# Order of a tile's two transposes in a mixture-of-experts stage: h transposed behind the next tile's first product

## What is computed

```python
def _L0_ffn_ref(x, gate_w, gate_b, bias, w1, b1, w2, b2):
    E, TOP_K, D, H = (8, 2, 512, 352)
    xf = x.reshape(-1, d)
    scores = xf @ gate_w.T + gate_b + bias
    top_scores, top_idx = jax.lax.top_k(scores, TOP_K)
    gates = jax.nn.softmax(top_scores, axis=-1)
    ...
    h = jax.nn.silu(jnp.einsum('td,ehd->teh', xf, w1) + b1)
    y = jnp.einsum('teh,edh->ted', h, w2) + b2
    out = jnp.einsum('ted,te->td', y, comb)
```

## Time and profile before

| | us |
|---|---|
| median of 3 runs (1011.74 to 1012.09) | 1011.93 |
| the profiled execution, whole | 1011.67 |
| its span in the trace | 1010.0 |
| PE busy | 996.3 |
| DVE busy | 686.4 |
| ACT busy | 514.0 |
| POOL busy | 259.3 |
| expert stage, first product of h(0) to the end | 815.7 to 1010.0 |

### The profile page before, as it was taken

The page is one execution under the profiler, slowest core; times in us unless marked ns, Lnnn a source line. Parts: engine busy times, 40 slices in busy tenths (PEclk is TensorE's granted clock), DMA queues, the critical chain, the costliest instruction groups (busy, mean ns, idle before and its releaser), DMA issues.

```text
span 1010.0 us, 17489 instructions
## 1 busy us (share of the span) xinstructions
PE 996.3 (99%) x5029; PEld 840.0 (83%) x5030; DVE 686.4 (68%) x1552; ACT 514.0 (51%) x1324; POOL 259.3 (26%) x413
## 2 busy tenths in 40 slices
PE   8999999999999999999999999999999989999998
PEld 7888888888888888888788888888888879988996
DVE  7888655565666667667877878777887665544544
ACT  4545444454444457755555555555554954343442
POOL 1000000000000002222423233333333645656564
PEclk9999999999999999999999999999999999999999
DMA  7002501000000011343221111111125635555653
GB/s 262 23 21 84 209 27 36 21 21 21 21 22 21 21 63 63 104 173 116 43 53 49 45 42 42 42 42 42 42 73 161 187 119 101 108 102 99 110 107 48
DMA packets 46861, 75.35 MB, mean 75 GB/s; under 512 B 6089, under 2 KB 18554, under 8 KB 46690
## 3 DMA queue, kind: packets, MB, share of 16 engines
q1 hardware_dynamic: 37010, 56.04, 18.0%
q0 software_dynamic: 9808, 18.79, 10.1%
HBM read 53.14 MB, written 23.50 MB: 76 GB/s over the span
## 4 chain that ended last, share of the span: by engine, by line
PE 93%; DVE 3%; ACT 2%; DMA 1%; issue 1%; SPq 0%; POOL 0%; POOLq 0%; DVEq 0%; ACTq 0%
PE pK L1614 16%; PE pK L1616 16%; PE pK L1615 16%; PE pA L1614 6%; PE pA L1616 6%; PE pA L1615 6%; PE pX L1614 6%; PE pX L1616 5%; PE pX L1615 5%; PE pA L1748 3%; PE pT L1958 2%; PE pT L1694 2%; PE pX L1976 1%; PE pA L1882 1%; DVE w_lo L1523 1%; PE pT L1629 1%
## 5 line engine op out<-in xcount | busy, mean ns | idle before, releaser
L965 ACT ACTIVATE qs<-q,nrec 128x64 f32<-128x64 f32 x512 | 129.6, 336 | 88.0 <-DVE nrec L1344 87.9
L586 POOL TENSOR_TENSOR wv_lo<-wv_in,wv_hi 128x512 fp32r<-128x512 f32 x4 | 5.2, 1292 | 403.0 <-ACT wo_hi L886 403.0
L1614 PE MATMUL pA<-k_hi,xn_hi 128*128 128x512 f32 x256 | 101.0, 394 | 0.5 <-DVE k_lo L1219 0.5
L1614 PE MATMUL pK<-wq_hi,xnT_hi 128*128 128x512 f32 x256 | 100.4, 392 | 0.0
L1614 PE MATMUL pK<-wk_hi,xnT_hi 128*128 128x512 f32 (+1 forms) x256 | 100.1, 391 | 0.2 <-DVE xnT_lo L1199 0.2
L1616 PE MATMUL pK<-wq_hi,xnT_lo 128*128 128x512 f32 x256 | 99.9, 390 | 0.0
L1616 PE MATMUL pA<-k_hi,xn_lo 128*128 128x512 f32 x256 | 99.8, 390 | 0.0
L1615 PE MATMUL pK<-wk_lo,xnT_hi 128*128 128x512 f32 (+1 forms) x256 | 99.7, 390 | 0.0
L1615 PE MATMUL pA<-k_lo,xn_hi 128*128 128x512 f32 x256 | 99.7, 389 | 0.0
L1616 PE MATMUL pK<-wk_hi,xnT_lo 128*128 128x512 f32 (+1 forms) x256 | 99.7, 389 | 0.0
L1615 PE MATMUL pK<-wq_lo,xnT_hi 128*128 128x512 f32 x256 | 99.7, 389 | 0.0
(11 more groups left out here) (277 smaller groups left out, 2447.7 us busy)
## 6 DMA issues: line engine op xcount, KB each, us to landing
w_in<-in_ffn_w SPq DMA_DIRECT2D x22, 256.0 KB, 3.6
w_in<-in_ffn_w SPq DMA_DIRECT2D x8, 704.0 KB, 7.6
xn<-in_attn_hidden_states SPq DMA_DIRECT2D x16, 256.0 KB, 6.3
wv_in<-in_attn_Wv SPq DMA_DIRECT2D x16, 256.0 KB, 2.8
wo_in<-in_attn_Wo SPq DMA_DIRECT2D x16, 256.0 KB, 3.0
wk_in<-in_attn_Wq SPq DMA_DIRECT2D x4, 1024.0 KB, 5.7
xnT_dram<-xnT SPq DMA_DIRECT2D x4, 1024.0 KB, 11.6
x_in<-in_attn_hidden_states SPq DMA_DIRECT2D x16, 256.0 KB, 2.6
```

Of the source, the lines that this page charges most:

```text
L965: i = nc.scalar.activation(qs[:, s], q[:, s], ACT.Copy, scale=nrec[:, b * HC + h:b * HC + h + 1])
L1614: nc.tensor.matmul(dst, lhs[0], rhs[0], start=start, stop=False)
```

## The change

In PE's order, hT(i-1) now stands behind h(i) and ahead of gT(i+1); it was hT(i) behind y(i-2). ACT's and DVE's orders follow: ACT takes the copy of h(i), the cast of gT(i+1), then silu of tile i-1. DVE takes gT_lo(i+1), hT_hi and hT_lo of tile i-1, then the scaling of y(i-2). PE's order is now: h(0), gT(1), h(1), hT(0), gT(2); then h(i), hT(i-1), gT(i+1), y(i-2); then h(38), hT(37), y(36), hT(38), y(37), y(38). The matmuls, copies and transfers are the same ones.

```diff
-            def act_tile_e(i, e=None, last=False):
-                act_h(i)
-                if not last:
-                    act_gT(i + 1)
-                if e is None:
-                    e = act.value_load(tile_expert[0:1, ds(i, 1)], min_val=0, max_val=E - 1)
-                act_silu(i, e)
+            def act_tile_e(i):
+                act_silu(i, act.value_load(tile_expert[0:1, ds(i, 1)], min_val=0, max_val=E - 1))
...
-            act_tile_e(0, first_expert)
-            with act.Fori(1, NS - 1) as i:
-                act_tile_e(i)
-            act_tile_e(NS - 1, last=True)
+            act_h(0)
+            act_gT(1)
+            act_h(1)
+            act_gT(2)
+            act_silu(0, first_expert)
+            with act.Fori(2, NS - 1) as i:
+                act_h(i)
+                act_gT(i + 1)
+                act_tile_e(i - 1)
+            act_h(NS - 1)
+            act_tile_e(NS - 2)
+            act_tile_e(NS - 1)
...
             with dve.Fori(2, NS // 2) as h:
                 for b in range(2):
                     dve_gT(2 * h + (b + 1))
+                    dve_hT(2 * h + (b - 1), 1 - b)
                     dve_y(2 * h + (b - 2), b, 16 * h - 16)
-                    dve_hT(2 * h + b, b)
+            dve_hT(NS - 2, 1)
             dve_y(NS - 3, 0, 16 * (NS // 2) - 16)
             dve_hT(NS - 1, 0)
             dve_y(NS - 2, 1, 16 * (NS // 2) - 16)
...
             pe_h(0, first_experts[0])
             pe_gT(1, 1)
+            pe_h(1, first_experts[1])
             pe_hT(0)
-            pe_h(1, first_experts[1])
             pe_gT(2, 0)
-            pe_hT(1)
             pe.wait_ge(w_lo_ready, len(DVE_STEPS))
             with pe.Fori(1, NS // 2) as h:
                 for b in range(2):
                     i = 2 * h + b
                     pe_h(i, expert(i))
+                    pe_hT(2 * h + (b - 1))
                     pe_gT(2 * h + (b + 1), 1 - b)
                     pe_y(2 * h + (b - 2), b, expert(2 * h + (b - 2)))
-                    pe_hT(i)
             pe_h(NS - 1, expert(NS - 1))
+            pe_hT(NS - 2)
             pe_y(NS - 3, 0, expert(NS - 3))
```

More of the change, by code:

```diff
@@ L1587, in _ @@
             dve_gT(1)
-            dve_hT(0, 0)
             put_gates()
             dve_gT(2)
-            dve_hT(1, 1)
+            dve_hT(0, 0)
             dve.wait_ge(gates_ready, 1)
@@ L1595, in _ @@
                 dve_gT(i + 1)
+                dve_hT(i - 1, 1 - i % 2)
                 dve_y(i - 2, i % 2, 0)
-                dve_hT(i, i % 2)
             with dve.Fori(2, NS // 2) as h:
```

## The result

The changed kernel takes **1013.77 us** (median of 22 runs, 1013.23 to 1015.15), the kernel before in the same comparison 1012.03 (22 runs, 1011.6 to 1012.81). The ratio is 1.0017, with a 95% interval of 1.0012 to 1.0023: +1.7 us where +0.7 was forecast. The profiled execution took 1013.59 us and spans 1011.9.

What follows compares the result with a forecast made beforehand. PE, dense with work between the pipeline's filling and its end, was taken to bound the kernel. Loop -0.3, start +0.34 and end +0.6 gave +0.65, rounded to +0.7 us: 1012.6 us from 1011.93, 8-in-10 range 1011.3 to 1014.0.

Steps and rivals of the forecast that it cites:

- the sum: Whole kernel: loop, start and end terms together +0.65, rounded to +0.7 us, from 0.0 to +1.5; chance 0.88.
- The start: PE's gap before gT(2): hT(0) leaves the first gap and delays the copy of h(1) and all up to h(2), +0.34 us.
- The seams: Transitions between PE's groups in each steady tile: all four cost at most 0.02 us of 4.78; -0.3 us taken over 36 tiles.
- Rival (b): PE's exit from transposes to products costs array time: one exit less gives 0.09 us a tile, 1009.7 us; chance 0.04.
- The loop: Steady tiles, h(3) to h(38): only the seams between PE's groups change the time, -0.3 us, between -0.7 and +0.2.
- The end: Behind h(38): hT(37) on the path +0.33, new wait before y(37) +0.45, wait before y(38) -0.2; +0.6 us, +0.3 to +1.0.
- The covers: Slack in the loop before PE would wait: 0.44 us for gT_lo ahead of h, 1.8 for hT_lo ahead of y; no cost.
- Rival (a): Every steady tile: gT_lo late for h(i+1), ACT's copy queued behind hT(i-1); 0.1 us beyond cover gives 1016.2 us; chance 0.07.
- Rival (c): Steady loop: seven grouped transposes lower PE's clock to 1.2 GHz, up to twice the 167 us, near 1180 us; chance 0.01.

## Why the prediction was right, and where it was not

**The outcome.** No difference above 0.2%, on the slower side, inside the range of 8 in 10: right, with the interval's upper end at 0.23%. The size was off, +1.7 us for +0.7, and that is above the sum's own bounds, +1.5 us or 1013.4. The range held because it was drawn wider than the sum, for mis-sized seams and handovers. Of what came, two parts had no term in the sum, a change of h's rhythm and a slow read on PE's sequencer, and that they stayed within the added width is luck.

**The start: right.** +0.35 us against +0.34. h(2)'s first product came at 824.32, forecast near 824.3. The two kernels in which hT(0) went back into the gap show it alone: 8.22 and 8.23 us from h(0) to h(2), before 8.21.

**The seams: right, at less.** The seams gave back 5 ns a tile, 0.17 us in all, where the forecast -0.3 is 8 ns a tile. Rival (b), a dear way out of transposes, fell with the period that it would have shortened: a tile is 4.79 us, not 4.69.

**The loop: the step that failed.** The term for the steady loop, -0.3 us between -0.7 and +0.2, was a sum of seams alone; measured is +0.54. It took h's spacing of 0.158 us from the one tile of the earlier trace rows and held it for given, whatever stands ahead of h. It isn't: ten steps took 1.58 to 1.61 us in the kernel before, by expert, and with a product or a single transpose ahead of h some tiles at odd places take 1.66. That made +0.71 us of the stretch in one execution and about +1.0 in the other. Shown are the two conditions: the kernel before with only the seam changed has slow tiles, three transposes ahead take them away, even places take them away, odd places for all experts spread them to experts of both kinds. What in the chip makes the rhythm, and why it takes one tile and spares the next, no run settles.

**The end: a mis-sized term.** With T the start of hT(37), 998.89, the reckoning holds nearly to its last step. PE was there at T + 2.76 (forecast 2.75), silu at T + 1.30 (1.2), hT_lo's end at T + 3.15 (3.05). But y(37) started at T + 3.62, not T + 3.2. The wait was 0.86 us and not 0.45: 0.1 from the silu, the rest the read of the expert number behind the wait for silu(37), which the prediction costed on ACT and left out on PE. The kernel with early reads puts it at 0.32. With a read of 0.3 us the omission would have cost nothing, as the two kernels with one transpose ahead show; the read took 0.68. hT(37) took its 0.33, and y(37) to y(38) went from 2.37 to 2.19, -0.18 for a forecast -0.2. Together 0.33 + 0.86 - 0.18 = +1.0, the upper bound of the term. The last scatter followed y_last's scaling by 0.78 us as before (1007.07 + 0.75 to 1008.60), so the reading of y_last in the prediction holds.

**The covers: right.** gT_lo ended at 852.60 and h followed at 853.17, with 0.57 between, 0.14 of it the handover: 0.43 of cover, forecast 0.44. The longer ACT chain gave 0.35 to 0.45. hT_lo's, from the changed kernel's DVE to the y(i-1) that reads it at 855.76, is 1.83 of a forecast 1.8:

```profile
851.91 0.69 DVE L1202 TENSOR_TENSOR gT_lo<-pT,gT_hi 128x512 fp32r<-128x512 f32 x1 [2.00 <-ACT gT_hi L1127]
...
853.37 0.56 DVE L1202 TENSOR_TENSOR hT_lo<-hT,hT_hi 128x384 fp32r<-128x384 f32 x1
```

Rival (a) was 0.43 us away.

**The clock: right.** The changed kernel from 829 to 1000 us (us, busy time of each engine, granted clock, DMA share, GB/s), seven transposes in a row in each tile:

```profile
829.00:1000.00 171.00, 171.00 (x1001) 156.27 (x1000) 82.35 (x143) 64.83 (x176) 89.76 (x69) 1.00 0.56 99
```

It is 1.00, and so is that of the kernel with ten transposes a tile. Rival (c) fell. The Trainium skill ("TensorE: Matmul & The Clock Gate", section "Part 4: PE-mode transpose") says that the full clock does not engage for transposes; in this kernel's loop the trace disagrees, with 1.00, as in the earlier trace rows. In all these stretches the clock was 1.00 before the transposes began, so whether transposes would bring it up from the lower level, no run here shows.

## What to carry to other kernels

When PE has no idle time, a reorder must be costed on its sequencer as well. What the sequencer reads for a group belongs ahead of any wait that may hold. Behind one, the read (0.30 us, at some places up to 0.94), its checks and the issue took 1.0 us from 855.1 to 856.10 in the kernel with one transpose ahead, and what the array has queued must cover it. A spacing read from one tile is not the loop's: compare the same ten steps over all tiles before you build on nanoseconds, and sort them by the operand's address. Undoing half of a reorder is a new order with waits of its own, as two experiments here showed.

## What the runs showed of the hardware

Products of 352 columns step at 0.158 us, 0.160 to 0.162, or 0.166. The step of 0.166 appeared only with the moving operand (w1) 128 bytes off a multiple of 256, counted from the start of w1, and never behind three transposes (no slow tile of 35 in each of three kernels; 5 to 17 where odd places follow a product or one transpose). Which of those tiles take it is open. One wait with one register read behind it, ahead of each h, cost 0.73 us a tile, 26 us in the stretch; the profile shows it under the name "issue" alone. Of the 78 reads of an expert number by PE's sequencer in the changed kernel, 72 took 0.30 to 0.32 us and six 0.49 to 0.94; in the kernel before, seven took 0.42 to 0.92. The long ones inside the loop left no wait of PE. ACT's copies out of PSUM in a row start 0.35 us apart though each is shown 0.45 long.
